# Weaving an FFN's shared products between its routing steps on TensorE, in a kernel of retention, oscillator and two FFN passes

## What is computed

```python
x = x + retention(norm(x))      # 4 layers, 8 heads, each with an MLP of 256
x = x + ffn(norm(x))
x = x + oscillator(norm(x))     # needs cos(t * freqs) and gamma ** t for t < 2048
x = x + ffn(norm(x))

def ffn(x):                     # 8 experts, hidden width 256
    shared_out = swiglu(x, shared_gate, shared_up, shared_down)
    logits = x @ gate_w.T
    top_id = argmax(logits); score = sigmoid(max(logits))
    routed = swiglu(x * score, r_gate[top_id], r_up[top_id], r_down[top_id])   # per token
    return shared_out + routed
# swiglu(x, g, u, d) = (silu(x @ g.T) * (x @ u.T)) @ d.T
```

## Time and profile before

| | us |
|---|---|
| median of 3 runs | 635.3 (634.47 to 635.82) |
| profiled execution, its own time | 634.63 |
| its span in the trace | 632.8 |
| PE, DVE, ACT, POOL busy | 557.3, 492.1, 357.5, 210.5 |
| granted TensorE clock, mean | 0.939 |

### The profile page before, as it was taken

The page is one execution under the profiler, slowest core; times in us unless marked ns, Lnnn a source line. Parts: engine busy times, 40 slices in busy tenths (PEclk is TensorE's granted clock), DMA queues, the critical chain, the costliest instruction groups (busy, mean ns, idle before and its releaser), DMA issues. The chain is left out here.

```text
span 632.8 us, 14034 instructions
## 1 busy us (share of the span) xinstructions
PE 557.3 (88%) x4376; PEld 428.2 (68%) x4376; DVE 492.1 (78%) x1825; ACT 357.5 (56%) x822; POOL 210.5 (33%) x218
## 2 busy tenths in 40 slices
PE   1899999999999999999877986985599996998884
PEld 1666778777877878877654755984256774867782
DVE  6899888888888888888886657678868999653453
ACT  2678877777877877877443655666043210123560
POOL 2344434433442442443400450563100000361552
PEclk9999999999999999999795679999699997698999
DMA  9949999990000000000002213113000000012215
GB/s 314 379 111 181 186 176 190 185 150 2 3 2 2 2 2 2 1 3 2 1 2 69 65 43 75 56 39 93 0 1 1 1 1 1 22 43 77 69 39 149
DMA packets 61129, 43.29 MB, mean 68 GB/s; under 512 B 4640, under 2 KB 58272, under 8 KB 60800
## 3 DMA queue, kind: packets, MB, share of 16 engines
q1 hardware_dynamic: 56160, 35.42, 27.9%
q0 software_dynamic: 2496, 5.13, 2.4%
q10 hardware_dynamic: 2400, 1.84, 0.9%
HBM read 18.38 MB, written 24.01 MB: 67 GB/s over the span
## 5 line engine op out<-in xcount | busy, mean ns | idle before, releaser
L462 POOL TENSOR_TENSOR att<-att,small 128x512 f32<-128x512 f32 x64 | 81.9, 1280 | 174.3 <-ACT att L359 174.3
L1003 POOL DMA_INDIRECT rows_back<-ffn_yt,ffn_front x46 | 46.5, 1010 | 62.4 <-DVE ffn_yt L1347 54.3
L367 ACT ACTIVATE xz<-resid,nmr,rs 128x128 f32<-128x128 f32 x128 | 56.7, 502 | 10.5 <-DVE nmr L810 10.5
L359 ACT ACTIVATE att<-banks 128x512 f32<-128x512 f32 x64 | 38.8, 607 | 41.1 <-PE banks L508 41.1
L1184 PE MATMUL banks<-ffn_xtT,ffn_wt 128*128 128x128 f32 x368 | 51.1, 283 | 12.1 <-DVE ffn_wt L1326 6.9
L1184 PEld LDWEIGHTS banks<-ffn_xtT,ffn_wt 128*128 128x128 f32 x368 | 45.5, 195 | 15.7 <-ACT ffn_wt L1058 9.0
L690 DVE TENSOR_TENSOR att<-banks,small 128x512 f32<-128x512 f32 x64 | 44.0, 687 | 10.5 <-PE banks L508 10.3
L508 PE MATMUL banks<-qexp,qkT 32*128 32x256 f32 x512 | 46.2, 430 | 3.6 <-DVE att L690 3.1
L480 POOL TENSOR_TENSOR qk<-cosq,sinq 128x512 f32<-128x512 f32 x32 | 40.8, 1276 | 13.9 <-DVE cosq L739 13.7
L994 POOL DMA_INDIRECT rows_in<-ffn_front,ffn_slot x32 | 32.1, 1005 | 38.5 <-DVE ffn_slot L1263 30.3
L559 PEld LDWEIGHTS banks<-w,hT 128*128 128x128 f32 x256 | 33.4, 204 | 12.6 <-issue 12.2
(11 more groups left out here) (259 smaller groups left out, 1467.0 us busy)
## 6 DMA issues: line engine op xcount, KB each, us to landing
rows_in<-zero_rows SPq DMA_DIRECT2D x16, 1032.0 KB, 18.7
shared_tab<-in_rot SPq DMA_DIRECT2D x3, 1024.0 KB, 12.0
routed_sb<-in_routed SPq DMA_DIRECT2D x1, 3072.0 KB, 13.2
ffn_front<-rows_in SPq DMA_DIRECT2D x46, 64.5 KB
ffn_yg<-rows_back SPq DMA_DIRECT2D x8, 256.0 KB, 3.6
shared_tab<-in_rot ACTq DMA_DIRECT2D x1, 1024.0 KB, 9.5
w<-in_W SPq DMA_DIRECT2D x2, 512.0 KB, 7.6
times<-in_times SPq DMA_DIRECT2D x1, 1024.0 KB, 5.2
```

The costliest lines, as they stand in the source:

```text
L359: act.activation(att[:, c, HALF:HEADS].rearrange("p (r e) n -> p r e n", e=PER_TILE), b_att[:, 2:4, c], ACT.Copy).then_inc(s["att_raw"], 1)
L367: ins = act.activation(xz[:, n], resid[:, (g % GROUPS) * 2 + n % 2], ACT.Identity, scale=rs[:, n:n + 1], bias=nmr[:, n:n + 1])
L462: pool.tensor_tensor(att[:, c, HALF:HEADS], att[:, c, HALF:HEADS], spread(causal.unsqueeze(1), 1, HALF), ALU.mult) \
L1003: pool.indirect_dma_start(rows_back, bass.IndirectOffsetOnAxis(ap=token, axis=0), yt[:, j % RING], None).then_inc(stored[j % RING], 16)
```

## The change

1. *PE, the front of both passes.* The four 512-column products of block 0 (quarters, `shared_quarter`) go one by one between a group's logits and its ranks. Behind the counts come gate and up of block 1, then in turn down of a block and gate and up of the block two further on, up to block 3. Both `keep_running` behind the shared blocks are gone (the one at the start stays). Logits of a group come ahead of later transposes.
2. *PE, the loop.* Down of block 2 is issued in step 0, behind the transpose of tile 0, down of block 3 in step 4. Ahead of the first routed product PE waits for DVE's last hidden product (`hs_ready` 4). Nothing of the shared expert is left behind the loop.
3. *DVE.* Each group is placed ahead of the next group's choice; `shared_hidden(0)` stands behind the last choice and ahead of `scaled(3)`. `shared_hidden(3)` comes ahead of the loop, the add of block 2 in step 2, the add of block 3 behind the remainders. The first reduction is two halves, ahead of and behind the first weights, the first of them behind POOL's last scatter (`ones_set` 2).
4. *ACT.* Doublings 0 to 9 move into steps 34 to 37 of the retention, doubling 10 to the head of the front; `one_half` moves ahead of POOL's last masks. A silu of one element at the end of the retention brings the table load there. Angles and turns are cut into quarters of 1024 columns and lie between the silus.

```diff
+                DOUBLED_BEFORE_H = {34: (0, 2), 35: (4, 6), 36: (7, 8), 37: (9, 10)}
+                DOUBLED_FIRST = {35: (2, 4), 36: (6, 7), 37: (8, 9)}
                 def step(t, u, on):
+                    first, last = DOUBLED_FIRST.get(t, (0, 0))
+                    tables.doubled(act, first, last)
...
                     if on(6):
                         g = t - 6
-                        wait(act, s["w1_ready"], g + 1)
                         wait(act, s["w2_ready"], g)
+                        first, last = DOUBLED_BEFORE_H.get(t, (0, 0))
+                        tables.doubled(act, first, last)
+                        act.wait_ge(s["w1_ready"], g + 1)
                         act.activation(hT[:].rearrange("p a b -> p (a b)"), b_xv, ACT.Gelu_apprx_tanh) \
...
                 run(step)(act)
+                act.activation(th[:, 0, 0:1], ve[:, 0, 0, 0, 0, 0, 0:1], ACT.Silu)
...
+        DOWN_IN_LOOP, ADDED_IN_LOOP = {0: 2, 4: 3}, {2: 2}
...
+                if tables:
+                    tables.doubled(act, 10, 11)
+                transposed(0)
+                transposed(1)
+                half_angle(0)
+                transposed(2)
+                if tables:
+                    tables.angle(act, 0, 1)
+                transposed(3)
+                half_angle(1)
+                if tables:
+                    tables.angle(act, 1, 3)
+                shared_silu(0)
+                half_angle(2)
+                if tables:
+                    tables.angle(act, 3, 4)
+                half_angle(3)
+                if tables:
+                    tables.turns_rounded(act)
+                    tables.turns_whole(act, 0, 1)
+                shared_silu(1)
+                if tables:
+                    tables.turns_whole(act, 1, 4)
+                shared_silu(2)
...
                 for t in range(AHEAD):
                     weights(t)
+                shared_silu(3)
...
-                shared_silu(LATE)
...
+                transposes(0)
+                logits(0)
+                transposes(1)
+                transposes(2)
+                shared_quarter(0, 0)
+                ranks(0)
+                transposes(3)
+                logits(1)
+                shared_quarter(0, 1).then_inc(s["gate_psum"], 1)
+                ranks(1)
+                logits(2)
+                shared_quarter(0, 2)
                 ranks(2)
+                logits(3)
+                shared_quarter(0, 3).then_inc(s["up_psum"], 1)
                 ranks(3)
                 counts()
+                shared_gate(1)
+                shared_up(1)
...
-                for b in range(LATE):
-                    if b + 1 < LATE:
-                        shared_gate(b + 1)
-                        shared_up(b + 1)
+                for b in range(2):
                     shared_down(b)
-                keep_running(pe, banks[:, 5, :], small, 2)
+                    shared_gate(b + 2)
+                    shared_up(b + 2)
+                pe.wait_ge(s["gate_silu"], NCH // BLK)
...
+                        if t == 1:
+                            pe.wait_ge(s["hs_ready"], NCH // BLK)
...
+                    if t in DOWN_IN_LOOP:
+                        shared_down(DOWN_IN_LOOP[t])
                 run(step)(pe)
-                pe.wait_ge(s["xtT_ready"], TILES)
-                shared_gate(LATE)
-                pe.wait_ge(s["hr_ready"], TILES)
-                shared_up(LATE)
-                shared_down(LATE)
...
+                for b in (1, 2):
                     chosen(b)
                     counted(b)
                     scaled(b)
                     placed(b)
+                chosen(3)
+                counted(3)
+                shared_hidden(0)
+                scaled(3)
+                placed(3)
                 tiles_known()
```

142 lines of the change are left out of this document (56 added, 86 removed).

## The result

The change is slower by a little: 637.47 us (median of 14 runs, 634.2 to 643.88) against 635.08 for the kernel before in the same series (14 runs, 632.45 to 635.95), a ratio of 1.0039 with a 95% interval of 1.0021 to 1.0057. The forecast was 625.1. The profiled execution took 642.38 us, its span is 640.6. It is not a typical one: eleven of the 14 lie at 634.2 to 639.0 us with a mean clock of 0.928 to 0.937, three at 642.4 to 643.9 with 0.909 to 0.912, and it is one of the three. So the table shows where those lose 7 to 8 us; how the others lose their 2 us no profile shows.

A forecast was written before the change was run, and what follows sets the result against it. It took PE, full because slow (clock 0.77 and 0.75), to bound the FFN fronts. Terms -4.0 (second pass), -8.2 (first), +0.3 (retention) gave -11.9; with +1.7 returning, -10.2: 625.1 us against the 635.3 median; range 621.5 to 637.0.

The forecast's parts named there:

- second pass, at full clock: Second front, part-by-part reckoning assuming full PE clock: groups of 3.1 us, first routed product at 572.3 against 577.55, -5.2 us.
- That rival: PE's clock stays at or falls to half in the weave: 634.2 us in one pass (chance 0.24), 643.3 in both (0.12).
- the two clock cases: Half clock in the weave in one pass, chance 0.24, or in both passes, chance 0.12.
- one pass at half: Half clock in one front's weave: +9.1 us there, -1.1 in all, 634.2 us; chance 0.24.
- both: Half clock in both fronts' weaves: +8.0 us in all, 643.3 us, slower than before; chance 0.12.
- one late signal: Fronts: before's two late signals counted as gone, one allowed to come back on the path, +1.7 us.
- the sign of being right: POOL's scatters in the fronts would show no gap over 0.4 us between them.
- The landing: SP's first load ahead of the loop lands in 2.6 us; late-landing rival 5.2 us, 630.3 us in all, chance 0.10.
- The loop and tail of the first pass: Loop: -3.3 us from the halved reduction, +1.8 for block 3's down product; behind the loop -1.4 on DVE.
- The tail's add: Behind the second pass's loop, the 0.68 us add between the last adds leaves the path: -0.6 us.
- Retention: Ten doublings move into ACT's pauses; all but one fit: +0.3 us, bounds 0 and +1.5.
- Block 3 in front of the loop: PE would end 2.3 us ahead of POOL and the landing; block 3's down product adds 1.8 us per loop.

The follow-up runs named there:

- held: The change plus six unread 512-column products, two behind the first transposes and one beside each quarter; 639.47 us, ratio 1.0064 to the kernel before.
- late3held: late3 plus the six unread products of held; 640.23 us, ratio 1.0042 to the kernel before.
- combo: The change with before's PE and DVE orders in fronts, loops and tails, keeping retention doublings, ACT's quarters and halved reduction; 636.10 us, ratio 1.0002 to before.
- late3: The change with all of block 3's work put back behind the loop in both passes, weave kept; 635.23 us, ratio 1.0014 to the kernel before.
- two_all: The change with two quarters in each group, all blocks ahead of the loop; 638.13 us, ratio 1.0003 to before; repeated at 634.77 us, ratio 1.0006.
- two_late3: late3 with two quarters of shared products in each group instead of one; 639.63 us, ratio 1.0043 to the kernel before.
- spaced2: latesc with 12 small POOL memsets behind each scatter, in one series with latesc2; 665.01 us, ratio 1.0475 to the kernel before.
- latesc: held with POOL's first scatter held back until all four groups have their slots; 651.12 us, ratio 1.0230 to the kernel before.
- latesc2: latesc repeated unchanged, in one series with spaced2; 651.99 us, ratio 1.0270 to the kernel before.
- spaced: latesc with 12 small POOL memsets behind each scatter, in a series where before took 619.02 us; 653.99 us, ratio 1.0561 to before.
- two_p4: two_all with 4 small POOL memsets behind each scatter; 615.83 us, ratio 0.9941 to the kernel before.
- two_p8: two_all with 8 small POOL memsets behind each scatter; 620.05 us, ratio 1.0007 to the kernel before.

## Why the prediction was wrong

- **The step that failed** is the first sentence of its second part: "second pass, at full clock". All of the fronts' terms (a group of 3.1 us, counts at 553.6, PE ready at 568.0, first routed product at 572.3) hang on it. Measured: half clock from 533.9 to 571.4 us and, in the first pass, from 349.6 to 376.9; groups of 5.6 to 6.3 us, PE ready at 582.3, first routed product at 584.3. That rival stood there with its price. In both passes it was to give 643.3 us against the median, 0.7 less against the profiled execution, and that one took 642.38; its groups were to take 5.4 us. The mistake was the chance, 0.50 for the forecast against 0.36 for the two clock cases, though the earlier trace rows had shown a fall under busy PE, and the only evidence for a full clock was one 0.9 us product in a group.
- **Where the median fell.** 637.5 lies between "one pass at half" (634.2) and "both" (643.3), and just above the range (637.0). The range ended where the one-pass case did, and that left the two-pass case wholly out.
- **The forecast for full clock was itself too low**, by a cause that it had in hand. It let "one late signal" come back at 1.7 us. With the clock held (held, late3held) DVE's waits for work that was done came to 2 to 4 us each, several in a pass, and the fronts stayed at 45 to 48 us. Only with a pause between the scatters, and in a series where before takes 620 us, was a front of 39.5 us seen.
- **POOL and the scatters**: never starved, 20.7 us from the first to the last, but the first came 2.1 us late, and the sign of being right (no gap over 0.4 us) was not met: three gaps have 0.8 to 1.0. **The load**: I had read its 2.2 us behind the last scatter as the price of a scatter's completion. In the second pass it was SP's reads of row numbers that ended last, before and in the change (3.8 us behind); that made no difference, since PE was later still. The landing was 1.9 us, not 2.6.
- **The loop and tail of the first pass**: -1.7 and -1.2 against -1.5 and -1.4. The loop's figure is luck, two errors that cancel: products 1 and 3 moved together by 2.0 us, not 3.3, and the rest of the loop grew by 0.4, not by 1.8. The other three profiles of the change have 42.4 to 42.5 us in this loop, 0.7 to 0.8 below before. combo shows besides that the reduction's part was not DVE's alone: the first half costs as much as it saves, unless PE has block 3 to do meanwhile. The second pass's loop: +1.0 for +1.8.
- **The tail's add**: 0 instead of -0.6 in the second pass. **Retention**: +0.3 forecast, -0.7 measured, within a spread of 3.7 us between profiles.
- **Block 3 in front of the loop** was costed at slack behind the landing of the load, which exists only at full clock. At half clock PE sets the end of the front, and so its 3.6 us were on the path. What they cost in all is less clear: late3 won 1.7 us back in a front at half clock and lost them behind it.

## What to carry to other kernels

A TensorE that is busy from end to end can still run at half clock. Here, with 512-column products spread one by one between transposes, logits and ranks, the clock stayed at half for 27 and 37 us (the change) or fell to it (late3); it came back under the four products of a block in one piece (6.2 us in the kernel before, 6.7 in the change), and with two in each group it was full for the ranks of all four groups in the first pass of two_all and of three in its second. Before weaving wide work into narrow, ask what brings the clock back in the old order, and whether the weave takes that apart. Then look at who else is at work in the stretch: beside indirect DMAs 1.26 us apart a handoff from TensorE to another engine came up to 5 us late in ordinary fronts (two_late3, two_all), and a kernel with a better clock (late3held, 0.963) was no faster than one with a worse (late3, 0.930). Spacing the DMAs took the lateness away in spaced2; whether a small pause makes a real kernel faster was not settled.

## What the runs showed of the hardware

- Signals of PE came 8 to 13 us late beside indirect scatters 1.26 us apart (64.5 KB each; latesc, latesc2), and not beside the same scatters 1.73 us apart (spaced2, on the chip of latesc2). PE's products stand in the trace at the same times in both. SP's reads were drawn out in the same way, 9.0 us for 4.3. What holds them up was not found. In latesc2 PE's clock fell at 384.8 us, ahead of the late add (387.1) and silu (391.4), which speaks against products that ran late.
- The kernel before took 634.8 to 637.3 us in four of the series and in the first comparison, and 619.0 and 620.7 in two series, one of them with the chip number of a series at 634.8. In those two no late signal was seen in any profile (spaced, two_p4, two_p8), but all three kernels have pauses between their scatters. Loops took 36 to 38 us in them where the other profiles have 40 to 45. No profile of the kernel before was taken there, and why the series differ is open.
- Memsets of POOL behind an indirect DMA cost about 0.04 us each when 12 follow one another (0.48 us), and move the next DMA from 1.26 to 1.73 us behind the last.
